# Twelve tiles of the second pass loaded ahead of it instead of four, in a three-pass convolution kernel

## What is computed

```python
def _gn(v, G=32, eps=1e-5):
    B_, C_, H_, W_ = v.shape
    g = v.reshape(B_, G, C_ // G, H_, W_)
    m = jnp.mean(g, axis=(2, 3, 4), keepdims=True)
    s = jnp.var(g, axis=(2, 3, 4), keepdims=True)
    return ((g - m) / jnp.sqrt(s + eps)).reshape(v.shape)

x = x + _L0_conv_ref(_gn(x), L0_conv_weight, L0_conv_bias)   # 8x8 blocks mixed by a 64x64 matrix
x = x + _L1_conv_ref(_gn(x), ...)
# _L1_conv_ref(x): h = batchnorm(x); h = sign(h); h = 3x3 conv of h with sign(w) * scale, 16 groups;
#                  h = batchnorm(h) + x; return where(h > 0, h, a * h)
```

## Time and profile before

| | |
|---|---|
| median of 3 runs | 4535.15 us (4534.61 to 4535.2) |
| the profiled execution's own time | 4534.77 us |
| its span, first to last instruction | 4533.0 us |
| busy: TensorE, VectorE, ScalarE, GpSimd | 94%, 92%, 84%, 32% |
| moved by DMA | 1612 MB, mean 356 GB/s over the span |
| pass 1 / pass 2 / pass 3, by the first work of each | about 0 to 1757, 1757 to 2760, 2760 to 4533 us |

### The profile page before, as it was taken

One profiled execution on the slowest core, in us unless ns is written; L12 is line 12 of the kernel. 1 busy time (PEld: TensorE's weight loads), 2 busy tenths in 40 slices (PEclk: granted clock), 3 DMA queues, 4 the chain that ended last, 5 costly groups with the idle time before them and its releaser, 6 DMA issues.

```text
span 4533.0 us, 80720 instructions
## 1 busy us (share of the span) xinstructions
PE 4257.5 (94%) x21700; PEld 2709.6 (60%) x21956; DVE 4171.3 (92%) x9974; ACT 3795.5 (84%) x5265; POOL 1469.2 (32%) x3476
## 2 busy tenths in 40 slices
PE   6999999999999998999999997999999999999998
PEld 5999999999999995444444443444444444444443
DVE  5999999999999998999999998999999999999998
ACT  7999999999999996777777775777777777777776
POOL 3888888888888884000000000000000000000000
PEclk9999999999999998999999998999999999999999
DMA  5999999999999998999999998999999999999998
GB/s 188 320 315 318 320 316 321 315 318 319 317 320 317 319 318 316 400 400 401 401 401 401 401 401 330 386 392 384 389 387 389 389 384 388 389 388 387 386 389 307
DMA packets 778198, 1612.15 MB, mean 356 GB/s; under 512 B 23666, under 2 KB 417650, under 8 KB 745394
## 3 DMA queue, kind: packets, MB, share of 16 engines
q1 hardware_dynamic: 778162, 1611.72, 97.8%
HBM read 940.55 MB, written 671.09 MB: 356 GB/s over the span
## 4 chain that ended last, share of the span: by engine, by line
PE 31%; DVE 22%; issue 12%; ACT 11%; POOL 9%; DMA 8%; SPq 4%; DVEq 1%; POOLq 0%; ACTq 0%
DVE ring_x L972 8%; DMA h_scratch<-ring_x 8%; DVE early L765 7%; PE psT L1124 5%; PE psT L1126 5%; PE psV L1033 4%; PE psV L1126 4%; PE psV L1124 4%; ACT ring_y L670 3%; DVE ring_z L756 3%; POOL ring_y L469 3%; ACT ring_z L670 3%; PE psT L1101 3%; ACT ring_x L625 2%; SPq L381 2%
## 5 line engine op out<-in xcount | busy, mean ns | idle before, releaser
L1033 PE MATMUL psV<-W0T,ring_gT 128*128 128x128 f32 x8192 | 1080.7, 275 | 48.1 <-issue 33.6
L1033 PEld LDWEIGHTS psV<-W0T,ring_gT 128*128 128x128 f32 x8192 | 1077.8, 192 | 33.3
L765 DVE BATCH_NORM_STATS2 early<-ring_z 128x6 f32<-128x128 f32 x4096 | 822.9, 274 | 0.0
L756 DVE SCALAR_TENSOR_TENSOR ring_z<-psV,x_r,ring_x 128x1024 f32<-128x1024 f32 x512 | 657.4, 1284 | 118.0 <-DVE early L765 76.7
L660 ACT ACTIVATE late<-ring_x,minus_b 128x512 f32<-128x512 f32 x1024 | 639.7, 708 | 1.0 <-PE psV L1126 1.0
L849 DVE BATCH_NORM_STATS2 h_tup<-ring_x 128x6 f32<-128x512 uint16 x1024 | 630.8, 679 | 0.5
L469 POOL TENSOR_SCALAR ring_y<-ring_z,u_r,u_nm 128x1024 f32<-128x1024 f32 x508 | 601.1, 1200 | 35.6 <-POOL gn L488 35.6
L576 ACT ACTIVATE ring_g<-ring_x,x_ms 128x1024 f32<-128x1024 f32 x512 | 585.4, 1143 | 0.0
L563 ACT ACTIVATE ring_gT<-psT 128x1024 f32<-128x1024 f32 x512 | 523.7, 1023 | 49.9 <-PE psT L1016 24.2
L1016 PE MATMUL psT<-ident,ring_x 128*128 128x128 f32 x4096 | 539.5, 275 | 3.9 <-ACT rank_lhs L582 0.4
L625 ACT ACTIVATE ring_x<-ring_x,bn_c 128x2048 f16<-128x2048 f32 x256 | 533.4, 2084 | 5.3 <-DVE bn_c L831 5.3
(11 more groups left out here) (161 smaller groups left out, 5689.7 us busy)
## 6 DMA issues: line engine op xcount, KB each, us to landing
ring_x<-in_x SPq DMA_DIRECT2D x128, 2048.0 KB, 8.7
y_scratch<-ring_y SPq DMA_DIRECT2D x128, 2048.0 KB, 13.1
ring_x<-y_scratch SPq DMA_DIRECT2D x256, 1024.0 KB, 10.7
out<-ring_x SPq DMA_DIRECT2D x256, 1024.0 KB, 14.9
h_scratch<-ring_x SPq DMA_DIRECT2D x256, 512.0 KB, 10.8
ring_y<-y_scratch SPq DMA_DIRECT2D x64, 2048.0 KB, 10.0
ring_z<-y_scratch SPq DMA_DIRECT2D x64, 2048.0 KB, 10.1
ring_g<-h_scratch SPq DMA_DIRECT2D x64, 1024.0 KB, 12.8
```

Of the source, the lines that this page charges most:

```text
L756: dve.scalar_tensor_tensor(out=ring_z[:, c % 2, cols], in0=psV[:, j % 2, :], scalar=x_r[:, s, j:j + 1], in1=ring_x[:, s, cols], op0=ALU.mu ...
L765: last = dve.bn_stats(z_tup[:, s, j, 2 * r:2 * r + 2, :].rearrange("p h t -> p (h t)"), ring_z[:, c % 2, SL * j + 2 * S * r:SL * j + 2 * S ...
L1033: last = pe.matmul(psV[:, j % 2, P * r:P * (r + 1)], ring_gT[:, j, P * r:P * (r + 1)], W0T[:, :], start=False, stop=(r % 4 == 3))
```

## The change

Four things are changed.

- `AHEAD = 12`: the first twelve tiles of y for pass 2 are loaded before it. Tiles 0 to 3 go to their slots in `ring_x` as before. Tiles 4 and 5 go to `ring_g` once all statistics of x are taken (`x_squared`), 6 and 7 to `ring_gT` once all products are made (`mixed`), 8 to 11 to `ring_z` once it has been counted (`z_counted`). Each has a semaphore of its own (`y2_early`).
- In the first 12 steps of pass 2 SP loads only at steps 0 to 3: tiles 12 to 15, into `ring_x`. Steps 4 to 11 issue no load, only the stores of words.
- From step 12 on a step is what it was: the sign of tile t is waited for and tile t + 4 loaded, then the words of tile t - 3 are stored.
- SP no longer waits for all stores of y ahead of pass 2; it does before it loads tile 16. The first loads wait for three stores of each slot instead of one.

`rounds` writes out 16 steps for SP and ScalarE instead of 8; TensorE and VectorE are as they were.

```diff
@@ -25,6 +25,7 @@
 FU = NQ * SL
 UNIT = NQ * (P // GROUPS)
 BANK = 512
+AHEAD = 12
 PAIRS = GC // 2
 HEAD = TAIL = 4
 SLOTS = 4
@@ -176,6 +177,15 @@
         def y2_slot(s):
             return ring_x[:, s // 2, 2048 * (s % 2):2048 * (s % 2) + 2048]
 
+        def y2_place(i, c):
+
+            if not (isinstance(i, int) and SLOTS <= SLOTS * i + c < AHEAD):
+                return y2_slot(c % SLOTS)
+            n = SLOTS * i + c - SLOTS
+            if n < SLOTS:
+                return (ring_g if n < 2 else ring_gT)[:, 2 * (n % 2):2 * (n % 2) + 2, :].rearrange("p s f -> p (s f)")
+            return ring_z[:, :, :].rearrange("p s f -> p (s f)")[:, 2048 * (n % SLOTS):2048 * (n % SLOTS) + 2048]
+
         def word_slot(s):
             return ring_x[:, 2, 1024 * s:1024 * s + 1024].bitcast(I32)
 
@@ -254,6 +264,7 @@
         bn1_routed = sem("bn1_routed")
 
         y2_loaded = [sem(f"y2_loaded{s}") for s in range(SLOTS)]
+        y2_early = [sem(f"y2_early{t}") for t in range(SLOTS, AHEAD)]
         signed = sem("signed")
         packed = sem("packed")
         conv_done = sem("conv_done")
@@ -358,22 +369,30 @@
 
             def load_y2(i, c):
 
-                s = c % SLOTS
-                sp.dma_start(y2_slot(s).rearrange("p (m f) -> p m f", m=4),
-                             row(y_chan[:, c % J], i + c // J)).then_inc(y2_loaded[s], 16)
+                early = isinstance(i, int) and SLOTS <= SLOTS * i + c < AHEAD
+                loaded = y2_early[SLOTS * i + c - SLOTS] if early else y2_loaded[c % SLOTS]
+                sp.dma_start(y2_place(i, c).rearrange("p (m f) -> p m f", m=4),
+                             row(y_chan[:, c % J], i + c // J)).then_inc(loaded, 16)
 
             sp.wait_ge(evicted, 4 * (B - 2))
-            sp.wait_ge(y_stored[0], 16)
-            sp.wait_ge(y_stored[1], 16)
+            for s in range(2):
+                sp.wait_ge(y_stored[s], 16 * (AHEAD // J))
             for c in range(SLOTS):
                 load_y2(0, c)
             loops1 = (B - SLOTS) // SLOTS
+            sp.wait_ge(x_squared, NQ * B)
+            load_y2(1, 0)
+            load_y2(1, 1)
             store_y(loops1, SLOTS - 2)
+            sp.wait_ge(mixed, NQ * B)
+            load_y2(1, 2)
+            load_y2(1, 3)
             sp.wait_ge(y_last, NQ)
             sp.dma_start(y_unit[B // 2 - 1, 1], ring_y[:, 1, :].rearrange("p (c f) -> p c f", c=GC)).then_inc(y_stored[1], 16)
 
-            for s in range(2):
-                sp.wait_ge(y_stored[s], 16 * (B // 2))
+            sp.wait_ge(z_counted, NQ * B)
+            for c in range(SLOTS):
+                load_y2(2, c)
 
             def store_h(i, c):
                 t = SLOTS * i + c
@@ -384,12 +403,19 @@
             def pass2(i, c):
                 t = SLOTS * i + c
                 if until(i, c, T2 - SLOTS):
-                    sp.wait_ge(signed, t + 1)
-                    load_y2(i, c + SLOTS)
+                    if not from_round(i, c, SLOTS):
+                        sp.wait_ge(signed, t + 1)
+                        load_y2(i, c + AHEAD)
+                    elif from_round(i, c, AHEAD):
+                        sp.wait_ge(signed, t + 1)
+                        if c % SLOTS == 0 and not from_round(i, c, AHEAD + 1):
+                            for s in range(2):
+                                sp.wait_ge(y_stored[s], 16 * (B // 2))
+                        load_y2(i, c + SLOTS)
                 if from_round(i, c, 3):
                     store_h(i, c - 3)
 
-            rounds(sp, pass2, T2, 2 * HEAD)
+            rounds(sp, pass2, T2, AHEAD + SLOTS)
 
             def load_3(i, c):
 
@@ -619,11 +645,16 @@
 
             def take_sign(i, c):
                 t, s = SLOTS * i + c, c % SLOTS
-                act.wait_ge(y2_loaded[s], 16 * (i + c // SLOTS + 1))
+                if not from_round(i, c, SLOTS):
+                    act.wait_ge(y2_loaded[s], 16)
+                elif not from_round(i, c, AHEAD):
+                    act.wait_ge(y2_early[t - SLOTS], 16)
+                else:
+                    act.wait_ge(y2_loaded[s], 16 * (i + c // SLOTS + 2 - AHEAD // SLOTS))
                 if from_round(i, c, 2):
                     act.wait_ge(packed, t - 1)
                 act.activation(sign_slot(c % 2).rearrange("p (a n b) -> p n a b", a=SIDE, n=2 * IMG),
-                               y2_slot(s).rearrange("p (n a b) -> p n a b", n=2 * IMG, a=SIDE),
+                               y2_place(i, c).rearrange("p (n a b) -> p n a b", n=2 * IMG, a=SIDE),
                                ACT.Sign, bias=bn1_c[:, c % J, 1:2], scale=bn1_c[:, c % J, 0:1]).then_inc(signed, 1)
 
             def unpack(i, c):
@@ -643,7 +674,7 @@
                 if from_round(i, c, 2):
                     unpack(i, c - 2)
 
-            rounds(act, pass2, T2, 2 * HEAD)
+            rounds(act, pass2, T2, AHEAD + SLOTS)
             last = (T2 - SLOTS) // SLOTS
             unpack(last, SLOTS - 2)
             unpack(last, SLOTS - 1)
```

## The result

The changed kernel takes 4544.65 us (median of 14 runs, 4543.24 to 4548.81), the kernel before 4534.5 us (14 runs beside them, 4533.22 to 4536.17). The ratio is 1.0022 with a 95% interval of 1.0014 to 1.003: 10.2 us slower, where +7.6 was forecast. The profiled spans differ by the same, 4543.2 against 4533.0 us.

The account below looks back on a forecast made before the run. Pass 2 was taken as bound by data moved at 400 GB/s, so DMA idle time counts: 13.2 us instead of 5.6 gives +7.6 us on 4534.77, plus 0.4 for the median, stated as 4542.6 us; range 4530 to 4549.

Parts of the forecast that it names:

- full gain: Pass 2: eight early loads of 2.62 us each all save time, 21 us gained, 4514 us; chance 0.02.
- What bounds: Pass 2 is bound by the amount of data at 400 GB/s; 5.6 us idle or lost around its start.
- step 1: Start of pass 2: first store of words queues behind all early loads and lands at 1793.3 instead of 1777.3.
- step 2: ScalarE's words of tile 4 wait for the first store of words; convolutions slip 9.1 us from tile 7.
- step 3: TensorE's clock falls to 0.50 during the 9.1 us wait, costing 2.8 us in the convolutions behind it.
- step 4: Tile 16 is loaded at 1814.3, 11.9 us later; DMA engines idle 13.2 us before saturation.
- step 5: End of pass 2: 13.2 us idle instead of 5.6 gives +7.6 us, 4542.6 us, a slowdown of 0.17%.
- later drain: Early queue drains slower, through store/load changes, 343 GB/s, or stores of words mixing with loads: 4544.3 to 4549 us; chance 0.32.
- the forecast's: Main case at the start of pass 2: stall and low clock, 4540 to 4544.2 us; chance 0.50.
- No stall: Start of pass 2: short store served beside the loads, 4.3 us gained, 4530.9 us; chance 0.06.
- a short hole: TensorE's wait before tile 7 under 5.5 us, at most 1.2 us lost, 4536.4; chance 0.10 shared with unchanged clock.
- a steady clock: TensorE's clock doesn't fall in the wait before tile 7: 4.8 us lost, 4540; chance 0.10 shared with shorter wait.

Follow-up runs that it names:

- the last one above: Changed kernel with stores of words ahead of loads of tiles 12 to 15, twelve places as a ring, lead spent tile by tile: 4530.41 us, 0.9991 of the kernel before.

## Why the prediction was right

The order of events was right; the range, 4530 to 4549, says little for it, since it took in all cases but the full gain. What speaks for the working is that its steps can be found in the trace one by one.

- *What bounds.* Right. The saturated rate is again 400 to 401 GB/s, and the idle time up to saturation accounts for the change: 9.5 us more by the windows, 9.4 by the stretch, 10.2 in time. Of the 10.2 us between the profiled spans, 0.35 lie ahead of the stretch and 0.5 behind it.
- *Transfers up to the first store (step 1).* Right in kind, 1.3 us short in size. 1793.3 was forecast for the landing; the words of tile 4 start at 1794.90, in a run whose pass 1 ended 0.35 later. 0.7 us of it is the rate, 386 GB/s from 1776 to 1796 and not the 400 I took, and 0.3 the pieces before 1776.
- *Who waits (step 2).* Right: the hole on TensorE was 10.6 us, 9.1 forecast; 1.3 of the difference comes from step 1. That it is this store is shown by the kernel with the four stores on another queue.
- *The clock (step 3).* Right: 0.50 from 1796 to 1800. Its price was 2.2 us in the trace (5.90 against 3.73 for tile 6) and 1.9 to 2.5 by the run with TensorE kept busy; 2.8 had been taken from two convolutions that began the pass. That was some 0.6 too much and hid part of the longer hole. The comparison with 5.5 us was no test: with the four stores on another queue a hole of only 3.47 us lowered the clock too (0.50 from 1804 to 1807), and the convolution behind it took 5.13 us instead of 3.73.
- *When saturation begins (step 4).* Tile 16 at 1815.32, 1814.3 forecast. Idle or lost 14.1 us from 1796 on, 13.2 forecast, and 0.7 of slow transfers from 1776 to 1796 on top. The step let the engines run at full rate from the first data of tile 16. They didn't:

```profile
1817.00:1818.00 1.00, 1.00 (x6) 0.49 (x5) 1.00 (x3) 1.00 (x1) 0.00 (x0) 1.00 0.91 143
1818.00:1819.00 1.00, 1.00 (x7) 0.48 (x5) 1.00 (x3) 0.87 (x1) 0.00 (x0) 1.00 0.96 319
1819.00:1820.00 1.00, 1.00 (x8) 0.56 (x7) 1.00 (x2) 0.57 (x1) 0.00 (x0) 1.00 0.99 229
```

The engines are busy for 91 to 99% of these 3 us, and the stretch lacks 1.3 us all the same.
- *The sum* fell short by 2.6 us, 1.0 of it slower transfers up to 1796 (step 1) and 0.9 the longer gap (step 4), which the slow start at tile 16 can account for. The remainder, 0.7 us between the windows and the time, is of the size of the runs' own spread. The last addition of step 5 has a slip: 4542.4 and 0.4 make 4542.8, not 4542.6.
- *The rivals.* By its number the result, 4544.65, falls just inside the later drain's case (4544.3 to 4549), which I gave 0.32, and 0.45 us outside the forecast's (up to 4544.2), with its 0.50. The interval (6 to 14 us) doesn't tell the two apart. Of the three losses that made up the later drain, one came: where loads and stores of words start beside each other, busy engines move little, at tile 16 as in the kernel before from 1770 to 1776 (1.3 us here, where 2.4 were priced); what causes it was not tested. The new meetings of stores of y with loads fall between 1756 and 1776, at 391, 406, 381 and 404 GB/s, without the loss that I had priced, and the slowest stretch of the drain above is 381, not 343. So the forecast's mechanism is what happened, with one term of the rival on top. No stall, a short hole, a steady clock and the full gain are excluded.

## What to carry to other kernels

Where a pass is bound by the amount of data, cost a prefetch by the idle time of the DMA engines that it fills, not by the loads it moves; here that was 5.6 us, not the 21 us of eight tiles. Look then at what stands behind the early loads in the same queue: a small store on which a buffer's reuse hangs should go first (four loads moved behind such stores took back the whole loss here). And spend a lead bit by bit before the end: used up at once it left a gap behind it, and kept to the end it left one there.

## What the runs showed that I had not expected

- A long row of loads from 1776 to 1796 moved 386 GB/s in the changed kernel; in the kernels that mix stores of words into the same stretch it is 395 (e.g. the last one above). The mixture alone isn't the reason: with eight tiles ahead stores of words are moved from 1776 to 1784 too, at 387 and 384. Loads alone also ran at 395 in the kernel before, from 1764 to 1770. What makes the difference stays open.
- A full queue holds up the engine that fills it: a store of words whose issue takes SP 0.51 us at 1815.75 takes 2.58 us as the first of them, and it was 14 us late before it was even issued (1768.2 to 1782.20).
- Small repairs moved the gap and left its size: with eight tiles ahead, with the four stores on another queue and with the wait for the stores of y moved, the step that was aimed at went as expected, and the time stayed that of the kernel before.
